# Attention with row maxima on one core: row scores thirteen steps ahead instead of twelve, maxima turned and sent a step earlier

## What is computed

```python
q = _lin(xn, Wq, bq).reshape(b, n, H, HD) / np.sqrt(HD).astype(np.float32)
k = _lin(xn, Wk, bk).reshape(b, n, H, HD)
score = jax.nn.softmax(jnp.einsum('bihd,bjhd->bhij', q, k), axis=-1)
v = _lin(xn, Wv, bv).reshape(b, n, R, HD)
out = jnp.einsum('bhij,bjrd->bihrd', score, v)
```

## Time and profile before

| what | value |
|---|---|
| median of three runs | 1229.66 us (1228.99 to 1229.75) |
| profiled execution, its own time | 1227.82 us |
| its span, first to last instruction | 1225.9 us |
| PE busy | 1168.6 us (95%) |
| POOL, DVE, ACT busy | 955.8 (78%), 950.6 (78%), 756.2 us (62%) |
| mean granted clock of PE | 0.981 of full speed |

### The profile page before, as it was taken

One profiled execution on the slowest core, in us unless ns is written; L12 is line 12 of the kernel. 1 busy time (PEld: TensorE's weight loads), 2 busy tenths in 40 slices (PEclk: granted clock), 3 DMA queues, 4 the chain that ended last, 5 costly groups with the idle time before them and its releaser, 6 DMA issues. The chain is left out here.

```text
span 1225.9 us, 27573 instructions
## 1 busy us (share of the span) xinstructions
PE 1168.6 (95%) x7997; PEld 542.7 (44%) x7997; DVE 950.6 (78%) x2128; ACT 756.2 (62%) x1461; POOL 955.8 (78%) x561
## 2 busy tenths in 40 slices
PE   4699999999999999999999999999999999968898
PEld 2144444444444444444444444444444444425675
DVE  7676788888888787878787888787878888767762
ACT  4066767666666766666666666666666666654443
POOL 5277898989899898988898989897978878873321
PEclk9599999999999999999999999999999999999999
DMA  5334444343444344444444443444444434330000
GB/s 129 109 65 97 94 98 105 88 103 88 109 97 106 82 95 93 99 91 95 99 91 107 94 105 79 109 98 97 97 97 96 95 81 99 68 70 1 18 26 26
DMA packets 55765, 107.14 MB, mean 87 GB/s; under 512 B 6144, under 2 KB 25056, under 8 KB 55728
## 3 DMA queue, kind: packets, MB, share of 16 engines
q0 software_dynamic: 18784, 67.70, 29.2%
q1 hardware_dynamic: 36162, 38.65, 9.9%
q10 hardware_dynamic: 782, 0.33, 0.1%
HBM read 22.51 MB, written 8.39 MB: 25 GB/s over the span
## 5 line engine op out<-in xcount | busy, mean ns | idle before, releaser
L1245 DVE TENSOR_REDUCE rowmax<-row_bank 128x1 f32<-128x512 f32 x1024 | 662.3, 684 | 185.0 <-PE row_bank L1052 180.8
L1196 ACT ACTIVATE prob<-col_bank 128x512 f32<-128x512 f32 x1024 | 554.6, 594 | 263.8 <-PE col_bank L1071 262.7
L1081 PE MATMUL out_bank<-prob,v_op 128*64 128x512 f32 x2048 | 534.5, 594 | 0.2 <-ACT prob L1196 0.2
L1355 POOL TENSOR_TENSOR addend<-prob 128x1024 f32<-128x1024 f32 x128 | 323.1, 2524 | 45.9 <-ACT prob L1196 45.9
L1355 POOL TENSOR_TENSOR quad<-prob 128x1024 f32<-128x1024 f32 x128 | 335.1, 2618 | 20.1 <-ACT prob L1196 20.0
L1052 PE MATMUL row_bank<-k_op,q_op 72*64 72x512 bf16 x2048 | 326.9, 387 | 13.4 <-DMA q_op<-q_parts 8.9
L1071 PE MATMUL col_bank<-q_op,k_op 74*64 74x512 bf16 x2048 | 317.1, 382 | 3.4 <-DMA q_op<-max_rows 2.4
L1071 PEld LDWEIGHTS col_bank<-q_op,k_op 74*64 74x64 bf16 x2048 | 118.0, 109 | 246.9 <-ACT prob L1196 208.1
L1052 PEld LDWEIGHTS row_bank<-k_op,q_op 72*64 72x64 bf16 x2048 | 122.5, 109 | 153.1 <-DVE rowmax L1245 54.9
L1081 PEld LDWEIGHTS out_bank<-prob,v_op 128*64 128x64 f32 x2048 | 152.9, 136 | 67.3 <-issue 8.0
L1360 POOL DMA_DIRECT2D quad<-addend x128 | 112.4, 878 | 77.4 <-POOL addend L1355 72.8
(11 more groups left out here) (202 smaller groups left out, 805.6 us busy)
## 6 DMA issues: line engine op xcount, KB each, us to landing
quad<-addend POOLq DMA_DIRECT2D x128, 512.0 KB, 5.4
k_op<-k_parts SPq DMA_DIRECT2D x64, 144.0 KB
q_op<-q_parts SPq DMA_DIRECT2D x192, 48.0 KB
v_op<-v_all SPq DMA_DIRECT2D x32, 256.0 KB, 5.9
q_parts<-along_parts SPq DMA_DIRECT2D x11, 192.0 KB, 2.1
k_parts<-along_parts SPq DMA_DIRECT2D x33, 64.0 KB, 2.1
out<-y_out SPq DMA_DIRECT2D x8, 256.0 KB, 2.3
q_op<-max_rows SPq DMA_DIRECT2D x64, 4.0 KB
```

Of the source, the lines that this page charges most:

```text
L1081: last = nc.tensor.matmul(out_bank[ih * VW:(ih + 1) * VW, :], v_op[slot // 2][:, t, :], outs.halves(prob[:, t, :])[:, :, ih, :], start=(t ...
L1196: nc.scalar.activation(prob[:, t, h * HALF:(h + 1) * HALF], col_bank[h][:, :], ACT.Exp).then_inc(exp_done, 1)
L1245: nc.vector.tensor_reduce(rowmax[:, parity, t, h:h + 1], row_bank[h][:, :], AX.X, ALU.max).then_inc(max_done, 1)
L1355: pool.tensor_tensor(dst, prob[:, 2 * k, :], prob[:, 2 * k + 1, :], ALU.add).then_inc(pair_done, 1)
```

## The change

Five numbers change, and the places of four jobs. `LEAD` becomes 13 steps. DVE splits the maxima one step earlier (pieces after half-steps 5 to 7 instead of 7 to 9, counted `2 * t + h`). PE turns them and ACT copies them in step 4 instead of 5, so that SP's send follows a step earlier. In slot 1 PE turns the pair in step 2 instead of 3, and ACT takes it in step 3 instead of 4; in slot 2 PE projects it in step 1 instead of 2, and ACT takes the projection in step 2 instead of 3.

```diff
-LEAD = TB + TB // 2
+LEAD = TB + 5
...
-                        if t == 5 and not (last and s == SLOTS - 1):
+                        if t == 4 and not (last and s == SLOTS - 1):
                             if s == 1 and along:
                                 pe.wait_ge(project.xnT_ready, G + 1)
...
-                        if along and (s, t) == (1, 3):
+                        if along and (s, t) == (1, 2):
                             pe.wait_ge(max_rows_ready, u + 1)
...
-                        if along and (s, t) == (2, 2):
+                        if along and (s, t) == (2, 1):
                             pe.wait_ge(mix_in_ready, u - 1)
                             project.qk(pe, G)
...
-                        if t == 5 and not (last and s == SLOTS - 1):
+                        if t == 4 and not (last and s == SLOTS - 1):
                             sent = s >= 1 or not first
...
-                        if along and (s, t) == (1, 4):
+                        if along and (s, t) == (1, 3):
                             project.take_turned(act, G)
...
-                        if along and (s, t) == (2, 3):
+                        if along and (s, t) == (2, 2):
                             for m in range(2):
                                 project.take_qk(act, G, m)
...
-                            if 7 <= 2 * t + h < 10 and not (last and s == SLOTS - 1):
-                                split_max(u + 1, (s + 1) % 2, 2 * t + h - 7)
+                            if 5 <= 2 * t + h < 8 and not (last and s == SLOTS - 1):
+                                split_max(u + 1, (s + 1) % 2, 2 * t + h - 5)
```

## The result

The changed kernel takes 1239.97 us, the median of five runs (1239.16 to 1242.50), against 1229.66 for the kernel before, also five (1227.89 to 1229.91). The ratio is 1.0090, 95% interval [1.0076, 1.0104]. That is 10.3 us slower. Forecast were 5.4 us, and a range that ended at 1238.8: the sign was right, the size half, and the time lies 1.2 us above the range. The profiled execution took 1239.16 us, its span 1237.3, 11.4 us over the span before.

The account below looks back on a forecast made before the run. PE was taken as the bound in the 64 units, with DVE about one step of slack. Terms 3.2+2.2+0.8-1.5+1.1-0.4=+5.4 us on the median 1229.66 gave 1235.0 us, 8-in-10 range 1229.6 to 1238.8.

Parts of the forecast that it names:

- The split in slots 0 and 3: Moved split pieces delay DVE's second maximum, so PE waits in step 4: +3.2 and +0.8 us (slot 3), +2.2 (slot 0).
- the first piece starts 0.04 us later: Price of the split's first piece on DVE, read after the maxima at 620.01: 0.04 us, then 0.16 to the next instruction.
- The split in slot 2: In slot 2 the shorter DVE work after the split was to leave PE no wait: 0, with 0.1 in 14 places for the range.
- 0.20 less leaves nothing: Slot 2's work after the split was taken as 0.33 us instead of 0.53, cancelling the 0.20 us wait of other slots.
- The sends: Sending the maxima one step earlier removes PE's five waits for them: -1.5 us, bounds -3 and 0.
- The start: One more tile before unit 0 starts it 1.42 us later, part regained through PE's clock: +1.1 us, range 0.7 to 2.1.
- The end: The last tile's row scores lie a step earlier, so one step loses 0.43 us: -0.4 us.
- The pair: The projected pair's transposes and projections only move between steps, with inputs ready 1.1 us in hand: 0.
- a step elsewhere grows: Sign of being wrong: a step outside the forecast places lengthens, above all steps 1 to 3 of slots 1 and 2.
- The split did not hide: Refers to the rival that DVE's queue swallows the moved split pieces: -0.8 us, 1228.9 us, chance 0.17.
- The seams did not shorten: Refers to the rival that earlier sends shorten each group's long first step, 15 times, 8.2 us: 1220.6 us, chance 0.05.
- The dear split: Rival: first piece 0.24 us in 25 places, 0.1 in slot 2, a later clock: 1239.4 us, chance 0.06.

## Why the prediction was right in sign and short in size

**The split in slots 0 and 3** (+6.2 forecast, +8.6 measured). The mechanism was right: the job behind the split is late, the second maximum with it, PE's second half with that, and the next step gives the lead back. The term that was mis-sized is the step "the first piece starts 0.04 us later, and the next instruction follows at 621.50, 0.16 us after that". That row comes from a place where the next job (L369) has no register instructions. At the new places it has them (in slot 0 with a short semaphore instruction behind them), and the split's start to the job takes 0.22 us (slot 3) and 0.23 (slot 0: 659.84 to 660.07), in slot 2 0.42:

```profile
659.84 0.17 DVE L1254 TENSOR_REDUCE max_parts<-rowmax 128x8 bf16<-128x16 f32 x1
...
660.07 0.25 DVE L181 BATCH_NORM_AGGREGATE along_moment<-along_stats 128x2 f32<-128x6 f32 x2
```

PE's hold came to 0.39, 0.27 and 0.27 us a place (slot 3 joint, slot 0, slot 3 plain) where the prediction had 0.32, 0.20 and 0.20. Most of the 0.07 more is the register instruction's: 0.06 in slot 3, 0.07 in slot 0, where the gap is 0.16 in group 0 without it. The steps grew by 0.03 more than the holds; why stays open.

**The split in slot 2** (0 forecast, +3.7 measured): the step that failed. "0.20 less leaves nothing" compared the jobs' lengths alone, and by the wrong job: L369 stands behind the split before the change (step 3 of slot 2), L362 behind the moved one (step 2). The lengths are alike, but L362 has two register instructions, 0.32 us, which lost their cover; 0.26 of that shows, 0.42 us to the job instead of 0.16. Without these 3.7 us the time would have lain inside the range. Two runs that removed just this, in different ways, gave the 3.6 us back. The orders ahead of the prediction had the hint: "L389 ISA" between L1255 and L389. I read it as a row without a price, since the views don't count such instructions as busy.

Of the 12.3 us that step 4 gained, 8.6 came back when the first piece went behind the job.

**The sends** (-1.5 forecast, about -1.6 measured, waits gone): right against the kernel before, with the seams taking their place as said. The reason was not known. The send of 835.72 took 4.4 us to PE's start because GpSimd had issued an accumulating transfer at 835.28, 0.44 us ahead of it: by the trace that transfer was in at 839.86 and the send at 839.89. The prediction held the Trainium skill's 2.0 us fixed cost ("DMA: Bandwidth & Descriptors", Anatomy of one DMA) against those 4.4 us and kept the gain. The page's figure is for GpSimd's queue, but it comes close here as well: in the twelve profiles the 97 sends of SP during which no packet of 1 KB or more was under way were in 1.73 to 1.89 us after their issue. So the late send did have another cause, as the prediction said it would by that page, and the gain came all the same. As the prediction did not know of the accumulations, that one step earlier was enough is in part luck. And the earlier send was worth more inside the changed kernel, 5.0 us, since the split's own delay pushes ten more sends behind an accumulation.

**The start** (+1.1 forecast, +1.2 measured, of which 0.2 is a later first maximum). Unit 0 begins 17.92 us after the first maximum, where it was 16.49: +1.43, forecast 1.42. In all three executions with twelve steps and all nine with thirteen these two figures stand. What the clock gives back can't be told. In the twelve profiles the granted clock rose from 0.50 to 1.00 (the 2.4 GHz level) 4.9 to 8.1 us after the start of unit 0, so the 5.9 us that the prediction read from one execution do not hold for others. From the first maximum to unit 1 it is 33.8 to 35.0 us with twelve steps and 34.6 to 36.3 with thirteen, medians 33.95 and 34.95. The Trainium skill's freely running monitor ("TensorE: Matmul & The Clock Gate", What's actually happening) is neither shown nor refuted by that.

**The end** (-0.4 forecast, -0.2): step 3 of unit 62 fell by 0.44, and step 4 took 0.21 back. **The pair** (0): right, by its own run.

**The signs and the rivals.** That "a step elsewhere grows" was one of the prediction's own signs of being wrong, and slot 2 gave it. The waits for DVE's maxima rose to 36, not to more than 40. The split did not hide. The seams did not shorten: plain groups' first step went from 1.72 to 2.28, as the prediction said against that rival. The dear split, 1239.4, came nearest, and at a chance of 0.06 it was given too little. Its 0.24 us for the first piece is close to the 0.22 and 0.23 measured, but its reason was a next maximum that cannot start as closely, not held registers, and its 0.1 in slot 2 was 0.26.

## What to carry to other kernels

A small instruction that waits for the one just ahead of it costs more than its length: everything behind it in that engine's queue stays back, register instructions too, which until then ran free under longer work (here 0.26 us at each of 14 places). Before moving such a wait, look in the order of instructions at what stands behind its new place, and put it behind the work that needs registers and not in front. And read holds of PE from the starts of its steps: the view of waits showed 3 us more here, of 11.

## What the runs showed of the hardware

*Register instructions are held by a wait on the same queue.* Shown on VectorE by two opposite edits: without them the gap is 0.16 us instead of 0.42, and with the waiting instruction behind them step 4 is back at 1.73. The same shows away from the split. In the changed kernel's profile 226 maxima wait more than 0.3 us for PE's row scores. During none of these waits did a register instruction begin; behind 194 of them one began 0.013 to 0.017 us after the maximum that had waited. The Trainium skill has two pages on it. "Vector Engine (DVE) Microarchitecture Reference", Instruction fetch and dispatch, has the sequencer issue an instruction's semaphore wait before it reads even the opcode; that the first of L362's two began 0.015 us after L1254, at 693.14, agrees. "Advanced Engine Details and Errata", Sequencer Loop, has an engine instruction pushed into a queue and wait for its semaphore there; read so, the register instructions could have run ahead, and the trace disagrees here.

*A small send behind a large accumulation lands with it.* At joint groups, a 4 KB send 0.18 us ahead of a 512 KB accumulating transfer was in after 1.82 us; 0.22 us behind, it was in after 4.50, 0.13 us after that transfer. The same holds for all 30 sends that PE waited for in five profiles: issued 0.09 to 1.27 us behind an accumulation, they were in 0.03 to 0.18 us after it. The 25 of them in slot 3 let PE go 4.7 to 5.0 us after the accumulation's issue, whether they had left 0.1 or 0.7 us behind it. The Trainium skill ("DMA: Bandwidth & Descriptors", Queues, rings and completion order) lets each DMA engine go round between queues packet by packet, but lets a semaphore's increment land only after every earlier write of that engine, across its queues. The trace agrees with the second at all 30 places. It agrees with the first at the place shown: the send's 16 packets of 256 bytes start from 456.78 to 458.54, the first ten in pairs some 0.33 us apart between packets of the accumulation, which start from 455.83 to 458.26. For the send of 835.72, 0.44 us behind, it does not show: there all 16 start at 839.32 or later, when the accumulation's last packet of 4 KB had started (839.15).

*Executions begin at different times.* The first maximum starts at 41.6 to 42.1 us in seven of the twelve profiled executions and at 44.2 to 45.2 in five; the kernels do not differ in what stands before it. What makes the difference was not looked at. Differences of a few us between single spans are therefore not the change's; the units are the steadier measure.
